# Attention edge sums of a graph network: four groups of weights on chip, exponents written and exponentiated in one buffer, a block's normalising moved behind the groups in two parts

## What is computed

```python
h = x @ Wn.T + bn
e = edge_attr @ We.T + be
xj = h[src]
a = leaky_relu(sum((xj + e) * attn, axis=-1), 0.01)
m = segment_max(a, dst)
a = exp(a - m[dst])
denom = segment_sum(a, dst)
out = relu(segment_sum(xj * (a / (denom[dst] + 1e-16))[:, None], dst))
x = layernorm(x + out)
```

## Time and profile before

| what | value |
|---|---|
| median of 3 timed runs | 3963.05 us (3957.98 to 3963.11) |
| the profiled execution | 3955.63 us |
| its span | 3953.9 us |
| the attention groups, 2414 to 3075 us of the span | 661 us |

### The profile page before, as it was taken

One profiled execution on the slowest core, in us unless ns is written; L12 is line 12 of the kernel. 1 busy time (PEld: TensorE's weight loads), 2 busy tenths in 40 slices (PEclk: granted clock), 3 DMA queues, 4 the chain that ended last, 5 costly groups with the idle time before them and its releaser, 6 DMA issues. The chain is left out here.

```text
span 3953.9 us, 83216 instructions
## 1 busy us (share of the span) xinstructions
PE 3150.0 (80%) x17737; PEld 2339.8 (59%) x17738; DVE 2445.3 (62%) x6400; ACT 1818.7 (46%) x6302; POOL 1231.8 (31%) x988
## 2 busy tenths in 40 slices
PE   5666666988987777989844435898999899999978
PEld 4444445888876665767633325787888444445455
DVE  7999998987876564235478877777766400001754
ACT  1888883344445552011299885777776000000111
POOL 1788888888888810111000000000000000002512
PEclk9999999999998898999955558999999999999989
DMA  2444445677878884767576654434332633541066
GB/s 97 126 122 121 121 121 117 183 216 225 243 240 272 271 298 147 219 202 211 166 222 203 195 164 122 145 118 132 106 100 73 203 131 123 186 149 54 0 236 242
DMA packets 438469, 654.85 MB, mean 166 GB/s; under 512 B 102637, under 2 KB 293742, under 8 KB 438244
## 3 DMA queue, kind: packets, MB, share of 16 engines
q1 hardware_dynamic: 351298, 519.69, 41.9%
q10 hardware_dynamic: 56434, 125.33, 8.9%
q0 software_dynamic: 30640, 8.64, 3.1%
HBM read 436.96 MB, written 215.57 MB: 165 GB/s over the span
## 5 line engine op out<-in xcount | busy, mean ns | idle before, releaser
L1072 POOL DMA_INDIRECT slots<-all_B,put_index x800 | 1044.0, 1305 | 341.6 <-issue 335.8
L2343 PE MATMUL gio_po<-gio_T,all_A 125*128 125x500 f32 (+1 forms) x1400 | 530.7, 540 | 6.0 <-DMA gio_T<-pair 6.0
L2343 PEld LDWEIGHTS gio_po<-gio_T,all_A 125*128 125x128 f32 x1400 | 249.8, 190 | 283.7 <-issue 276.9
L1326 ACT ACTIVATE lm_raised<-lm_hot,srt_words 128x125 f32<-128x125 bf16 x1200 | 353.0, 384 | 56.0 <-DVE lm_top L1240 40.6
L1043 PE MATMUL put_ps<-put_right_in,put_left_in 128*128 128x125 f32 x2210 | 319.3, 294 | 65.0 <-ACT put_left_in L900 64.4
L2090 PE MATMUL att_ps<-att_right,att_left 128*125 128x125 f32 x2380 | 312.5, 285 | 70.4 <-ACT att_right L2111 56.9
L1360 PE MATMUL lm_ps<-lm_v,lm_node 125*128 x1220 | 170.5, 184 | 236.6 <-issue 81.8
L1644 PE MATMUL c_po<-c_halves,c_T 125*125 125x512 f32 x1250 | 327.6, 411 | 19.9 <-DMA c_T<-counts 10.2
L2090 PEld LDWEIGHTS att_ps<-att_right,att_left 128*125 128x125 f32 x2380 | 284.4, 191 | 94.5 <-issue 85.0
L1043 PEld LDWEIGHTS put_ps<-put_right_in,put_left_in 128*128 128x128 f32 x2210 | 281.4, 202 | 89.2 <-ACT put_left_in L900 75.0
L2164 DVE SCALAR_TENSOR_TENSOR att_power<-soft_negated,srt_words,att_far 128x125 f32 (+1 forms) x1190 | 320.1, 344 | 3.7 <-ACT att_right L2111 3.3
(11 more groups left out here) (440 smaller groups left out, 5265.7 us busy)
## 6 DMA issues: line engine op xcount, KB each, us to landing
c_T<-counts SPq DMA_DIRECT2D x255, 312.5 KB, 3.3
pair<-put_T ACTq DMA_DIRECT2D x125, 625.0 KB
att_ring<-hot SPq DMA_DIRECT2D x480, 160.0 KB
gio_T<-pair SPq DMA_DIRECT2D x60, 1250.0 KB, 5.7
hot<-put_hot SPq DMA_DIRECT2D x448, 160.0 KB
all_A<-in_edge_attr_dram SPq DMA_DIRECT2D x100, 448.0 KB
lm_planes<-src_rows SPq DMA_DIRECT2D x123, 320.0 KB, 3.8
counts<-put_T ACTq DMA_DIRECT2D x125, 312.5 KB
```

Of the source, the lines that this page charges most:

```text
L1072: nc.gpsimd.indirect_dma_start(slots, bass.IndirectOffsetOnAxis(index[:, C * g + j:C * g + j + 1], 0), stage[:, C * g + j, :], None).then_ ...
L1326: ins = nc.scalar.activation(raised[:, j % 2, c * P:(c + 1) * P], hot[:, j, c * S:c * S + P], ACT.Copy, scale=logit[:, ds(G * g + c, 1)])
L2343: ins = t_.matmul(po[:, i % 2, h, 0:w], A[:, b, 128 * h:128 * h + 128], tiles, start=(b == 0), stop=(b == NB - 1))
```

## The change

`right` grows to four groups (`DEEP` = 4) and DVE writes its exponents straight into the group's place in it; ACT takes the exponential in that place. `power` and the semaphore `right_ready` are gone: PE waits for `left_ready` alone, and DVE may write a place once PE has used the group four before (`slot_free`). ACT does all five exponentials of group g + 1 behind the five casts of group g, where it took casts and exponentials by turns. `take(d - 2)` moves behind ACT's last casts of block d. DVE runs the chain of block d - 2 (now L2246 to L2253) after its last STT of block d and ahead of the copy of the tiles. The chain's last two instructions, which need the square root, become a part of their own (`scale`, L2262 and L2263) that runs one block later, ahead of the next chain; the square root moves to the start of ACT's next block.

```diff
-        left, right = s.sb("left", [L, PARTS, W, P]), s.sb("right", [L, PARTS, W, P])
+        DEEP = RING
+        left, right = s.sb("left", [L, PARTS, W, P]), s.sb("right", [L, DEEP * PARTS, W, P])
+        slot = (lambda r, f: right[:, ds(PARTS * r + f, 1), :, :].rearrange("p a w n -> p (a w) n"))
...
-        left_ready, right_ready, used = (s.steps(n, PARTS, PARTS, head=1) for n in ("left", "right", "used"))
+        left_ready = s.steps("left", PARTS, PARTS, head=1)
+        used = s.steps("used", PARTS, PARTS, head=DEEP)
...
+        def slot_free(eng, g, f):
+
+            eng.wait_ge(used.sem(f), g + 1)
...
+                        r = pe.snap(g % DEEP, min_val=0, max_val=DEEP - 1)
                         for f in range(PARTS):
                             left_ready.after(pe, g, f)
-                            right_ready.after(pe, g, f)
...
+                                                left[:, f, c, :], slot(r, f)[:, c, :],
...
-                        if attention:
-                            powered.after(act, g, f)
-                            nc.scalar.activation(right[:, f, :, :], power[:, f, :, :], ACT.Exp).then_inc(right_ready.sem(f), 1)
+
+                def exponents(g):
+                    r = act.snap(g % DEEP, min_val=0, max_val=DEEP - 1)
+                    for f in range(PARTS):
+                        powered.after(act, g, f)
+                        nc.scalar.activation(slot(r, f), slot(r, f), ACT.Exp)
...
-                    widen(g0)
-                    if n == 2 and by_dst:
+                    if not isinstance(d, int):
+                        hooks["act"](act, d - 3)
+                    exponents(g0)
+                    with act.Fori(g0, g1 - 1) as g:
+                        widen(g)
+                        exponents(g + 1)
+                    widen(g1 - 1)
+                    if n == 2:
                         take(d - 2)
-                    with act.Fori(g0 + 1, g1) as g:
-                        widen(g)
                     tiles_full(act, g1)
                     tiles_free(act, d, n)
                     nc.scalar.copy(T[h][:, 0:half, :], tiles_of(ps)[:, 0:half, 0:P]).then_inc(moved, 1)
-                    if n == 2 and by_dst:
-                        hooks["act"](act, d - 2)
...
+                    r = dve.snap(g % DEEP, min_val=0, max_val=DEEP - 1)
                     for f in range(PARTS):
-                        right_ready.freed(dve, g, f)
+                        slot_free(dve, g, f)
                         for c in range(W):
                             q = W * f + c
-                            ins = v.scalar_tensor_tensor(power[:, f, c, :], negated[:, ds(d, 1), :].rearrange("p a n -> p (a n)"),
+                            ins = v.scalar_tensor_tensor(power(r, f)[:, c, :], negated[:, ds(d, 1), :].rearrange("p a n -> p (a n)"),
...
                     with dve.Fori(g0, g1) as g:
                         attend(d, g)
+                    if not isinstance(d, int):
+                        hooks["scale"](dve, d - 3)
+                    if n == 2:
+                        hooks["dve"](dve, d - 2)
                     tiles_full(dve, g1)
                     tiles_free(dve, d, n)
                     if by_dst:
                         v.tensor_copy(T[h][:, half:NB, :], tiles_of(ps)[:, half:NB, 0:P]).then_inc(moved, 1)
-                        if n == 2:
-                            hooks["dve"](dve, d - 2)
                         return
...
+        def scale(dve, d):
+            v = nc.vector
+            r, mv, sd, rs = (b[n][:, :] for n in ("r", "mv", "sd", "rs"))
+            chain = Chain(dve, scaled, 2 * d)
             dve.wait_ge(rooted, d + 1)
             chain(v.reciprocal(rs, sd))
             chain(v.tensor_scalar(row(X, d), r, mv[:, 0:1], rs, ALU.subtract, ALU.mult))
```

More of the change, by code:

```diff
@@ L2021, in phase_weighted @@
             logit, negated = attention
-            far, power = s.sb("far", [L, 2, G * S], bf16), s.sb("power", [L, PARTS, W, P])
+            far, power = s.sb("far", [L, 2, G * S], bf16), slot
             measured, powered = s.sem("measured"), s.steps("powered", PARTS, PARTS, head=1)
-        rights_read = measured if attention else right_ready.sem(PARTS - 1)
+        rights_read = measured
         def blocks(eng, step):
@@ L2085, in step @@
                         units = at.pair()
+                        r = pe.snap(g % DEEP, min_val=0, max_val=DEEP - 1)
                         for f in range(PARTS):
                             left_ready.after(pe, g, f)
-                            right_ready.after(pe, g, f)
                             for c in range(W):
-                                ins = t_.matmul(tiles_of(ps)[:, ds(units[(W * f + c) // HALF], HALF), :][:, (W * f + c) % HALF, 0:P], left[:, f, c, :], right[:, f, c, :],
+                                ins = t_.matmul(tiles_of(ps)[:, ds(units[(W * f + c) // HALF], HALF), :][:, (W * f + c) % HALF, 0:P],
+                                                left[:, f, c, :], slot(r, f)[:, c, :],
                                                 start=False, stop=False, skip_group_check=True)
@@ L2126, in step @@
                     nc.scalar.copy(T[h][:, 0:half, :], tiles_of(ps)[:, 0:half, 0:P]).then_inc(moved, 1)
-                    if n == 2 and by_dst:
-                        hooks["act"](act, d - 2)
                 left_ready.begin(act)
-                if attention:
-                    right_ready.begin(act)
                 blocks(act, step)
                 act.drain().then_inc(left_ready.sem(PARTS - 1), RING)
-                if by_dst:
-                    for d in (NB - 2, NB - 1):
-                        take(d)
-                        hooks["act"](act, d)
+                hooks["act"](act, NB - 3)
+                for d in (NB - 2, NB - 1):
+                    take(d)
+                    hooks["act"](act, d)
             @block.vector
@@ L2194, in _ @@
                     measure(0)
-                else:
-                    right_ready.begin(dve)
                 blocks(dve, step)
                 dve.drain().then_inc(rights_read, RING)
-                if by_dst:
-                    for d in (NB - 2, NB - 1):
-                        hooks["dve"](dve, d)
-                else:
-                    for f in range(2):
-                        added.freed(dve, NB - 1, f)
-                    add(NB - 1)
-                    hooks["done"](dve)
+                hooks["scale"](dve, NB - 3)
+                for d in (NB - 2, NB - 1):
+                    hooks["dve"](dve, d)
+                    hooks["scale"](dve, d)
             @block.gpsimd
@@ L2214, in phase_attended @@
 def phase_attended(nc, k, H, X, scratch, attention):
-    PER = 9
+    PER = 7
     def make(s):
@@ L2220, in make @@
         sums = s.sb("sums", [P, D + 1])
-        varied, rooted, chain_sem, passed, finished = (s.sem(n) for n in ("varied", "rooted", "chain", "passed", "finished"))
+        varied, rooted, chain_sem, passed, finished, scaled = (
+            s.sem(n) for n in ("varied", "rooted", "chain", "passed", "finished", "scaled"))
         def rows(act, d):
@@ L2244, in dve @@
             chain(v.tensor_scalar(ve, mv[:, 1:2], EPS, None, ALU.add))
+            assert chain.n == PER, chain.n
             dve.sem_inc(varied, 1)
+        def scale(dve, d):
+            v = nc.vector
+            r, mv, sd, rs = (b[n][:, :] for n in ("r", "mv", "sd", "rs"))
+            chain = Chain(dve, scaled, 2 * d)
             dve.wait_ge(rooted, d + 1)
@@ L2248, in dve @@
             chain(v.tensor_scalar(row(X, d), r, mv[:, 0:1], rs, ALU.subtract, ALU.mult))
-            assert chain.n == PER, chain.n
             dve.sem_inc(finished, 1)
@@ L2259, in pool @@
             pool.wait_ge(totalled, NB + 1)
-        return {"pool": pool, "rows": rows, "act": act, "dve": dve, "start": lambda dve: None}
+        return {"pool": pool, "rows": rows, "act": act, "dve": dve, "scale": scale, "start": lambda dve: None}
     phase_weighted(nc, k, "att", True, H, D + 1, None, make, attention, scratch)
```

## The result

The changed kernel takes 4005.1 us (median of 4 runs, 3995.9 to 4014.5) against 3962.4 (3958.0 to 3963.1): ratio 1.0103, 95% interval 1.0088 to 1.0117. It is slower by 43 us; the forecast was 17, and its range ended at 3999. Its profiled execution has a span of 4002.9 us.

The account below looks back on a forecast made before the run. It took DVE to bound every attention block. Block 0 +11.0, block 1 +6.2, block 2 +3.0, blocks 3 to 11 +3.1, small blocks -3, end -1.2: +19, taken as +17 on 3963, so 3980 us; range 3950 to 3999.

Parts of the forecast that it names:

- What bounds the kernel: Attention stretch: DVE on the path in every block; PE's sequencer spaces fed groups 3.0 us; three-group blocks could win only 0.35.
- What goes: Between DVE's copy and the next `measure`: 5.5 us shrink to 0.05, as the bounds' loads move behind the copy.
- A longer tail: From DVE's last STT to the copy: grows from 1.95 to 5.3 us, waiting for ACT's last casts, `take` and the chain.
- Dearer addresses: DVE's STTs: more register operations stretch their pitch from 0.260 to 0.294 us, adding 0.49 a group.
- PE rival: PE becomes the limit: fed groups 3.4 us, small blocks 20.1, +10 in place of -3; +29 in all, 3992; chance 0.13.
- PE: PE's loop: one wait fewer, six operations a matmul, not three; fed group 3.2 us, not 3.0; hidden except in three-group blocks.
- The sum for the small blocks: Three-group blocks: PE needs 19.4 us (19.3 taken), DVE 18.9, against 19.55 before; -3 over twelve blocks.
- the group's 4.04: DVE's time for a group within a block: 3.55 us before plus 0.49 for addresses.
- register work free: Rival on DVE's STTs: added register work costs nothing, groups stay 3.55 us; -8 to -24 us, 3939 to 3955; chance 0.18.
- half: Rival on DVE's STTs: added register work costs 0.25 us a group; -1 in all, no change, 3962; chance 0.17.

Follow-up runs that it names:

- run 8: The kernel before with only the normalising moved: chain and scaling in two parts ahead of DVE's copy; 3949.6 us, ratio 0.9959.
- run 7: The kernel before with exponentials written to two places by turns, no wait altered, so each matmul's address takes 6 register operations, not 3; 4028.9 us, ratio 1.0160.
- run 12: The kernel before with the normalising moved ahead of the copy, fixed STT operands, exponential before cast, PE waiting for the cast alone; 3934.7 us, ratio 0.9929.
- run 2: The changed kernel with `measure` run for the group at hand, not one group earlier, so SP's report is needed one group later; 4002.0 us, ratio 1.0086.
- run 5: The kernel before with exponents written to two buffers by turns, giving STTs the changed kernel's register operations, no wait altered; 4013.3 us, ratio 1.0127.
- run 6: The kernel before with STT operands at fixed addresses (logits copied to a fixed tile, one fixed `far`), so no register instructions; 3974.7 us, ratio 1.0029.
- run 1: The changed kernel with SP reporting a ring slot as arrived one step earlier, before it waits for the casts and reloads; 4004.5 us, ratio 1.0101.
- run 4: The changed kernel with ACT's exponentials and casts by turns, each block's first group ahead of the loop; 3971.7 us, ratio 1.0016.
- run 9: The changed kernel with fixed tiles for logits and `far`, leaving each STT one register instruction of 3 or 4 operations; 3960.9 us, ratio 0.9997.
- run 3: The changed kernel with ACT's exponentials and casts by turns, all inside the loop; 4017.0 us, ratio 1.0137.

## Why the prediction was wrong, point by point

- **What bounds the kernel** (DVE in every block, little to win in the small ones): right, by the earlier trace rows and by run 8. Its cause for PE's 3.0 was half of it: "its sequencer is the limit" fits run 7, but ACT's ten instructions stand at the same 3.0 (run 12).
- **What goes**: the 5.5 between copy and `measure` went, to 0.1 and 0.6 and not 0.05: +7 us. What fills the 0.6 stays open.
- **A longer tail**: 5.2 against 5.3, `take` behind ACT's own casts; the tails' sum hit 82. The parts are off against each other: the first cast starts 0.5 behind the last STT, not 0.7. In block 1 the tail is 5.9, against 4.1 in run 2: PE's work there ran at a granted clock of 0.50 (0.75 in the stretch), a part of the PE rival that did come.
- **Dearer addresses**: right in kind and nearly in size, 0.46 a group against 0.49, and proved alone by run 5. The reason given, a sequencer without lead, was right (its 0.257 is the spacing in the trace; 2.2 / 8.5 by the printed digits is 0.259); run 6 adds that the engine's own pace is no shorter.
- **PE**: 0.40 a part and six operations, hidden as forecast. The sum for the small blocks (PE 19.4, DVE 18.9) had it wrong side up: PE needs 18.9 there (11.1 for product and zeroing, groups 2.26 and 3.2 apart, 2.3 for the last), since the first two groups stand ready and follow each other by 2.26 and not 2.5. DVE bounds them, 19.4 on average, 19.0 in run 1.
- **The step that failed** is the group's 4.04, which is 3.55 + 0.49: it keeps the 0.45 ahead of each `measure`, and puts at nothing what the later casts do to it. The part on the longer tail followed the casts behind the exponentials to `take`, to the chain and to PE. They have one more reader, SP, which waits for them before it reloads a slot and before it reports the next one, and DVE's `measure` waits for that report. The code says so in three lines, and the trace of before has SP's rows, with 0.6 to 1.1 us to spare; the forecast uses none of them. It cost 22 us in the gaps (11 of them in blocks 3 to 11, where a gap is 0.76 and not 0.45); some 7 by the casts' place behind the exponentials (run 4), the rest mostly where casts wait for PE behind a product, and how that rest divides is not shown. 16 of the forecast in the stretch + 23 (22 and the 1 that it took off) + 7 for copy to `measure` - 5 for the bodies is 41, as measured. Without the late reports the time would have been near 3983, inside the range.
- **Rivals**: register work free or half is refuted by run 5. PE as the limit is refuted as a bound of the small blocks (its recorded "+10 in place of -3" is +7 by its own 20.1, and 10 more than the forecast's -3); PE's granted clock fell to half at eight places, which goes with the longer tail of block 1 and with two of the ring's stalls. No rival gave 4005, and that is why the range missed: it took in bounds of the costs that were seen, and none for a wait that was not followed.

## What to carry to other kernels

When an instruction moves on one engine, list every semaphore that it raises and follow each to its readers, the queue that only issues transfers among them. A report that stands behind a wait in an in-order queue is as late as that wait, even for data that has landed. A queue that was always early shows in no engine's wait, but its own rows say by how much it was early: compare that with how far the change moves what it waits for. Before an operand gets an address from a register, set the sequencer's time for an instruction against the engine's own pace: here it was free up to there, and paid in full beyond. A reordering inside a loop can also move a table load into it. And where a change has several parts, run them apart: here one part was worth 14 us, and two others cost 50 and 22.

## What the runs showed of the hardware

- An STT of 128 x 125 fp32 with a bf16 operand starts 0.260 after the last with no register operation (run 6), three or four (run 9) or eight (before) ahead of it, and 0.293 with eleven or twelve (changed, run 5).
- On PE, an address of six operations costs 0.51 a part with two waits (run 7) and 0.40 with one (changed); one of three operations costs 0.36 with two waits (before) and 0.25 with one (run 12). So even a wait that is long met takes about 0.1 of the sequencer's time.
- An exponential as the loop's first table function cost a table load of 1.28 us in each turn, 103 loads for 23 (run 3); only the two blocks whose loops follow nothing but exponentials had none.
- PE's granted clock fell to 0.50 for 3.4 or 6.8 us at eight places of the changed stretch; in the 4 us ahead, PE was busy for 1.8 to 2.1 at seven of them and for 0.7 at one. With the gaps gone (run 1) blocks 3 to 24 ran at 1.00, though PE waited 1.4 us ahead of the last group of a block of five, as in the changed kernel; blocks 0 to 2, with longer gaps there, ran in part at 0.50 (0.74 in block 0).
